# A graph attention layer on one core: row buffers by parity in the sorting stage, and squares a tile at a time at the end

## What is computed

```python
# x (6250, 96) f32; src, dst (200000,) int32, ordered by dst; W* (96, 96); 4 heads of 24
q = (x[src] @ qW).reshape(e, 4, 24)
k = (x[dst] @ kW).reshape(e, 4, 24)
v = (x[dst] @ vW).reshape(e, 4, 24)
scores = clip(einsum('ehd,ehd->eh', q, k), -10, 10)
w = exp(scores) / (segment_sum(exp(scores), src)[src] + 1e-8)
res = segment_sum(w[:, :, None] * v, src).reshape(6250, 96)
out = layernorm(x + (x + res))        # over 96, eps 1e-5, no scale
```

## Time and profile before

| | us |
|---|---|
| median of 3 runs | 1888.74 |
| lowest, highest | 1873.3, 1890.82 |
| the profiled execution | 1897.0 |
| its span in the trace | 1895.2 |

### The profile page before, as it was taken

One profiled execution on the slowest core, in us unless ns is written; L12 is line 12 of the kernel. 1 busy time (PEld: TensorE's weight loads), 2 busy tenths in 40 slices (PEclk: granted clock), 3 DMA queues, 4 the chain that ended last, 5 costly groups with the idle time before them and its releaser, 6 DMA issues.

```text
span 1895.2 us, 56765 instructions
## 1 busy us (share of the span) xinstructions
PE 1554.5 (82%) x19964; PEld 1487.2 (78%) x19965; DVE 1485.0 (78%) x2939; ACT 1238.9 (65%) x1747; POOL 979.3 (52%) x762
## 2 busy tenths in 40 slices
PE   4845777777777777777775799999999999999990
PEld 3734777777777677777765799999999999999990
DVE  6888677777776777677751699999999999999987
ACT  3342444444444444444443799999999999999981
POOL 6231555555555655555555355555555555555550
PEclk8657888898898988888887899999999999999995
DMA  5673777777777777777675976777777777777731
GB/s 174 216 269 142 269 272 270 273 277 278 276 291 271 291 284 281 268 276 276 271 272 210 333 242 226 246 242 239 237 239 241 241 242 240 238 239 241 242 126 51
DMA packets 159447, 464.98 MB, mean 245 GB/s; under 512 B 36994, under 2 KB 59266, under 8 KB 152244
## 3 DMA queue, kind: packets, MB, share of 16 engines
q1 hardware_dynamic: 123572, 301.16, 48.7%
q0 software_dynamic: 35840, 163.36, 21.4%
HBM read 271.21 MB, written 209.73 MB: 254 GB/s over the span
## 4 chain that ended last, share of the span: by engine, by line
PE 64%; DMA 14%; DVE 8%; issue 6%; ACT 4%; POOL 2%; SPq 2%; ACTq 0%; POOLq 0%; DVEq 0%
DMA sorted_rows<-work 13%; PE two_a L1088 12%; PE meta L1150 11%; PE sum_bank L1150 11%; PE two_b L1088 10%; PE two_a L1171 6%; PE two_b L1171 6%; ACT work L875 3%; PE one_d L1161 3%; PE one_c L1161 3%; POOL sorted_rows L615 2%; SPq L798 1%; DVE cols_work L1271 1%; DVE work L1197 1%; DVE work L1204 1%
## 5 line engine op out<-in xcount | busy, mean ns | idle before, releaser
L615 POOL DMA_INDIRECT sorted_rows<-work x448 | 472.6, 1055 | 426.4 <-issue 327.1
L676 POOL TENSOR_TENSOR work<-work 128x768 f32<-128x768 f32 x236 | 448.4, 1900 | 359.7 <-ACT work L912 359.7
L921 ACT ACTIVATE work<-work 128x1024 f32<-128x1024 bf16 x236 | 501.1, 2123 | 0.0
L1088 PE MATMUL two_a<-work 128*128 128x192 bf16 x2688 | 310.8, 275 | 194.3 <-ACT work L875 194.2
L1088 PEld LDWEIGHTS two_a<-work 128*128 128x128 f16 x2688 | 250.8, 109 | 222.0 <-ACT work L875 207.2
L1088 PE MATMUL two_b<-work 128*128 128x192 bf16 x2688 | 301.2, 270 | 0.0
L1088 PEld LDWEIGHTS two_b<-work 128*128 128x128 f16 x2688 | 257.0, 108 | 9.3
L875 ACT ACTIVATE work<-two_a 128x768 f32<-128x768 f32 x224 | 180.6, 806 | 106.1 <-PE two_a L1088 106.1
L1150 PE MATMUL sum_bank<-work 128*128 128x100 f32 x1888 | 235.3, 278 | 1.7 <-DVE acc L1503 1.5
L1150 PE MATMUL meta<-work 128*128 128x100 f32 x1888 | 235.3, 278 | 0.8 <-DVE acc L1503 0.8
L1534 DVE TENSOR_REDUCE work<-work 128x32 f32<-128x768 f32 x236 | 225.0, 953 | 8.2
(11 more groups left out here) (229 smaller groups left out, 2357.1 us busy)
## 6 DMA issues: line engine op xcount, KB each, us to landing
work<-sorted_rows SPq DMA_DIRECT2D x472, 392.0 KB, 3.5
work<-sorted_local SPq DMA_DIRECT2D x56, 1024.0 KB
sorted_rows<-pad_rows SPq DMA_DIRECT2D x49, 392.0 KB, 4.6
work<-kv_table SPq DMA_DIRECT2D x112, 144.0 KB, 2.2
sorted_rows<-work POOLq DMA_INDIRECT x448
kv_table<-work SPq DMA_DIRECT2D x12, 576.0 KB, 3.4
work<-in_x SPq DMA_DIRECT2D x12, 192.0 KB, 3.8
out<-acc SPq DMA_DIRECT2D x4, 576.0 KB
```

Source lines behind the costliest of these rows:

```text
L615: pool.indirect_dma_start(out=rows_dram, out_offset=bass.IndirectOffsetOnAxis(ap=place_now[:, u, b:b + 1], axis=0), in_=payload[:, u, b * ...
L676: pool.tensor_tensor(now[:, :, 0:D].rearrange("p c (h f) -> p c h f", h=HEADS), blk[:, k, :, :, D:2 * D].rearrange("p m c (h f) -> p (m c) ...
L921: act.activation(hot_f[:, k % HOTF], hot[:, k % HOTS].rearrange("p n c -> p c n"), ACT.Copy).then_inc(hotf_made[k % PSEM], 1)
L1088: mm = pe.matmul(to, picked[:, u % 2, k * P:(k + 1) * P], window[:, u, :, n, :], start=(n == 0), stop=(n == 2))
```

## The change

payload, place_now and the scattered semaphores get one copy for even and one for odd steps; sorted_v gets 8 slots in place of 4; the loops write out two steps a turn, so that the parity p is known when the kernel is built. `moved_out` waits for the scatters of step c - 2. Three semaphores go (edge_pads, flag_made, local_kept), and their signals go to dve_step or away. Scratch arrays of stage 1 move in the shared SBUF tensor to make room. At the end: chunks of 15, 14, 12 and 8 tiles in place of 12, 12, 12 and 13; POOL divides chunks 2 and 3; ACT squares tile by tile with -mean as bias and the sum in accum_out; the reciprocal is taken before the root, chunk by chunk; and the mean's subtraction and the scaling are one instruction a tile. The order of the chunks is interleaved between DVE and ACT.

```diff
-        payload, at = share(0, [QUAD, NCH, WROW], F32)
+        payload, at = share(0, [2, QUAD, NCH, WROW], F32)
...
-        sorted_v, at = share(at, [4, QUAD, TW], F32)
+        sorted_v, at = share(at, [8, QUAD, TW], F32)
...
-        place_now, at = share(at, [QUAD, RB], F32)
+        place_now, at = share(at, [2, QUAD, RB], F32)
...
-        scattered = sems("scattered", QUAD)
+        scattered = [sems(f"scattered{p}_", QUAD) for p in range(2)]
...
-            with eng.Fori(4, NQ - 1) as a:
-                emit(eng.snap(a), eng.snap(a - 1), eng.snap(a - 3))
+            with eng.Fori(2, NQ // 2 - 1) as i:
+                for p in range(2):
+                    a = eng.snap(i * 2 + p)
+                    emit(a, eng.snap(a - 1), eng.snap(a - 3), 1 - p)
+            emit(NQ - 2, NQ - 3, NQ - 5)
...
-        def moved_out(eng, u, c):
-
-            if not zero(c):
-                eng.wait_ge(scattered[u], times(eng, c, 16 * RB))
+        def moved_out(eng, u, c, p):
+
+            if not (isinstance(c, int) and c < 2):
+                eng.wait_ge(scattered[p][u], times(eng, c, 8 * RB, -8 * RB * p))
...
-                        out=rows_dram, out_offset=bass.IndirectOffsetOnAxis(ap=place_now[:, u, b:b + 1], axis=0),
-                        in_=payload[:, u, b * RUN:(b + 1) * RUN, :].rearrange("p k w -> p (k w)"), in_offset=None,
-                        bounds_check=last_place, oob_is_err=False).then_inc(scattered[u], 16)
+                        out=rows_dram, out_offset=bass.IndirectOffsetOnAxis(ap=place_now[:, p, u, b:b + 1], axis=0),
+                        in_=payload[:, p, u, b * RUN:(b + 1) * RUN, :].rearrange("p k w -> p (k w)"), in_offset=None,
+                        bounds_check=last_place, oob_is_err=False).then_inc(scattered[p][u], 16)
...
-                with pool.Fori(0, NQ) as c:
-                    fast(c)
+                with pool.Fori(0, NQ // 2) as i:
+                    for p in range(2):
+                        fast(pool.snap(i * 2 + p), p)
...
+            pool.wait_ge(stat_made, STAT_INV)
+            for c in DIVIDED:
+                divide(pool, c).then_inc(divided, 1)
...
+            def squares(c):
+
+                lo, hi = CHUNKS[c]
+                act.wait_ge(stat_made, STAT_MEAN[c])
+                for t in range(lo, hi):
+                    act.activation(sq_all[:, t, :], acc[:, t, 0:D], ACT.Square, bias=stat[:, 1, t:t + 1],
+                                   accum_out=stat[:, 2, t:t + 1]).then_inc(square_made, 1)
+
+            def root(c):
+                lo, hi = CHUNKS[c]
+                act.wait_ge(stat_made, STAT_VAR[c])
+                act.activation(stat[:, 4, lo:hi], stat[:, 3, lo:hi], ACT.Sqrt).then_inc(square_made, 1)
+
+            squares(0)
+            squares(1)
+            root(0)
+            squares(2)
+            root(1)
+            squares(3)
+            root(2)
+            root(3)
...
+            def variances(c):
+                lo, hi = CHUNKS[c]
+                dve.wait_ge(square_made, SQUARES[c])
+                link(dve.tensor_scalar(stat[:, 3, lo:hi], stat[:, 2, lo:hi], 1.0 / D, EPS_LN, ALU.mult, ALU.add))
+                dve.reciprocal(stat[:, 3, lo:hi], stat[:, 3, lo:hi]).then_inc(stat_made, 1)
+
+            def normed(c):
+                lo, hi = CHUNKS[c]
+                dve.wait_ge(square_made, ROOTS[c])
+                for t in range(lo, hi):
+                    y = acc[:, t, 0:D]
+                    ins = dve.tensor_scalar(y, y, stat[:, 1, t:t + 1], stat[:, 4, t:t + 1], ALU.add, ALU.mult)
+                    ins.then_inc(y_made, 1)
+
+            means(0)
+            means(1)
+            variances(0)
+            means(2)
+            normed(0)
+            variances(1)
+            means(3)
+            normed(1)
+            variances(2)
+            normed(2)
+            variances(3)
+            normed(3)
```

More of the change, by code:

```diff
@@ L108, in gnn_program @@
     assert FULL + NT <= NBLK and FULL <= 512 and PIECES == 7 and TI == 12 and COLS * P <= 2048
-    CHUNKS = [(NT * c // 4, NT * (c + 1) // 4) for c in range(4)]
+    CUTS = (0, 15, 29, 41, NT)
+    CHUNKS = list(zip(CUTS, CUTS[1:]))
+    DIVIDED = (2, 3)
     kv3 = nc.dram_tensor("kv3_table", (NTAB, 3 * 2 * D), BF16).ap()
@@ L256, in gnn_program @@
         flag_f, at = share(at, [1], F32)
+        parts3, at = share(at, [2, TSLOT, 3, 3, D], BF16)
+        last3, at = share(at, [3, 3, D], BF16)
+        zeros_b, at = share(at, [3 * 2 * D], BF16)
+        weights, at = share(at, [3 * D], F32)
+        select_h, at = share(at, [LO, 2, UP], F16)
+        group_h, at = share(at, [LO, HG], F16)
+        low_row, at = share(at, [LO, HG * COLS], F16)
+        diag, at = share(at, [ITERS], F32)
         assert at <= MOVE_END
@@ L600, in _ @@
             pool.wait_ge(tails_out, 16 * NT)
-            pool.memset(payload[:, :, :, TAG + 1:WROW], 0.0).then_inc(pads_made, 1)
+            pool.memset(payload[:, :, :, :, TAG + 1:WROW].rearrange("p o u c w -> p (o u c) w"), 0.0).then_inc(pads_made, 1)
             pool.wait_ge(pads_made, 2)
@@ L659, in slow @@
                         pool.sem_inc(pool_turn, 1)
-                    scatter(u, at_c)
+                    scatter(u, at_c, p)
             with pool.If(over == 0):
-                with pool.Fori(0, NQ) as c:
-                    fast(c)
+                with pool.Fori(0, NQ // 2) as i:
+                    for p in range(2):
+                        fast(pool.snap(i * 2 + p), p)
             with pool.Else():
-                with pool.Fori(0, NQ) as c:
-                    slow(c)
+                with pool.Fori(0, NQ // 2) as i:
+                    for p in range(2):
+                        slow(pool.snap(i * 2 + p), p)
             def weigh(j, drain=False):
@@ L702, in _ @@
                 sp.dma_start(weights[0:D, n * D:(n + 1) * D], w).then_inc(loads, 16)
-            sp.wait_ge(edge_pads, 2)
+            sp.wait_ge(dve_step, 2)
             for flat, held in ((src, edge_i), (dst, dest_i)):
@@ L862, in _, with emit @@
             act.activation(q3[0:NREST, FULL_NT], last3[0:NREST, 2], ACT.Copy).then_inc(q_kept, 1)
-            def emit(a, b, c):
+            def emit(a, b, c, p=None):
                 if c is not None:
+                    p = parity(c, p)
                     done_c = counts(act, c, G2, 1)
-                    at_c = bass.ds(low_bits(act, c, 3), 1)
+                    at_c = bass.ds(low_bits(act, c, 7), 1)
                 def rows(u):
-                    moved_out(act, u, c)
-                    act.activation(payload[:, u, :, TAG], sorted_v[:, at_c, u, 0:NCH].rearrange("p o w -> p (o w)"),
+                    moved_out(act, u, c, p)
+                    act.activation(payload[:, p, u, :, TAG], sorted_v[:, at_c, u, 0:NCH].rearrange("p o w -> p (o w)"),
                                    ACT.Copy).then_inc(tag_kept[u % GSEM], 1)
@@ L1401, in place @@
                     group_done(dve, dest_made, u, done_c)
-                    moved_out(dve, u, c)
+                    moved_out(dve, u, c, p)
                     with nc.allow_low_precision(reason="whole numbers below 2**24"):
-                        dve.tensor_reduce(place_now[:, u], dest_ps[:, u], AX.X, ALU.add).then_inc(place_made[u % GSEM], 1)
+                        dve.tensor_reduce(place_now[:, p, u], dest_ps[:, u], AX.X, ALU.add).then_inc(place_made[u % GSEM], 1)
                 def quad_of(t, q):
@@ L1542, in _, with means @@
             link(dve.tensor_scalar(inv, acc[:, 0:NT, D:AW], EPS_W, None, ALU.add))
-            link(dve.reciprocal(inv, inv))
+            dve.reciprocal(inv, inv).then_inc(stat_made, 1)
+            dve.wait_ge(stat_made, STAT_INV)
             dve.wait_ge(loads, 48 + 32)
-            for lo, hi in CHUNKS:
+            def means(c):
+                lo, hi = CHUNKS[c]
                 y = acc[:, lo:hi, 0:D]
-                y4 = y.rearrange("p t (h f) -> p t h f", h=HEADS)
-                link(dve.tensor_tensor(y4, y4, inv[:, lo:hi].unsqueeze(3).to_broadcast([P, hi - lo, HEADS, DH]),
-                                        ALU.mult))
+                if c in DIVIDED:
+                    dve.wait_ge(divided, DIVIDED.index(c) + 1)
+                else:
+                    link(divide(dve, c))
```

84 lines of the change are left out of this document (33 added, 51 removed).

## The result

The changed kernel takes 1708.99 us (median of 4 runs, 1703.4 to 1711.48), the kernel before 1887.72 beside it (4 runs): a ratio of 0.906, 95% interval 0.901 to 0.911. The forecast was 1688 us with a range of 1636 to 1772. The profiled execution took 1711.48 us (span 1709.3), to be set against 1897.0 (span 1895.2) before: 185.9 us of span less, where the prediction's sum was 201.

What follows compares the result with a forecast made beforehand. The prediction took a ring of one row buffer per group to bound the sorting stage, then the DMA engines. Gains 181 + 15.5 - 1.5 + 6 = 201 us off 1888.7 gave 1688 us, range 1636 to 1772.

Steps and rivals of the forecast that it cites:

- The cause: Sorting stage: one row buffer per group makes copy, issue, flight and refill follow each other, 15.48 us a step.
- The next bound: Sorting step with second buffers: DMA engines largest at 11.6 us, with POOL 11.3, DVE 10.8 to 11.3, PE 10.3.
- Rival (b): Sorting: transfers keep up and DVE is the bound, 10.8 to 11.5 us a step; 1636 us at 11.0; chance 0.23.
- Rival (d): Sorting: the wait only changes its name, pace within 0.4 us of 15.48; 1870 to 1889 us; chance 0.04.
- Rival (e): Sorting: DVE's fast f16 instructions hold up POOL's scatter issues, 16.9 us a step; 1941 us; chance 0.04.
- The pace: 52 sorting steps: 12.0 us each instead of 15.48, range 11.0 to 13.5, a gain of 181 us.
- rival (c): Sorting: transfers fall behind, packets or window loads land late, 12.6 to 14.2 us a step; 1766 at 13.5; chance 0.19.
- The three last steps: End of sorting: DVE and brow's load gone, POOL sets 10.6 us a step instead of 15.75, gaining 15.5 us.
- The last landing: End of sorting: the last scatters land behind a fuller queue, costing 1.5 us of the gain.
- The loops: Sorting loops written out two steps a turn: 0 us a step, bounds -0.2 and +0.2.
- The end: After the last addition to acc: work leaves DVE, ACT squares tile by tile; gain 6 us, bounds 0 and 9.
- POOL's division is hidden: At the end: POOL's division of chunks 2 and 3 takes 2.9 us, ready by 1857, needed at 1862.7.

Runs made afterwards that it cites:

- run 1: Changed kernel, but each write of a row or place buffer waits for the scatters of the step before, not two before; 1908.63 us, ratio 1.009.
- run 3: Changed kernel with half the bytes in each scatter, as many issues, sums left out; 1661.02 us.
- run 5: Changed kernel loading only an eighth of brow from step 2 on, sums not the right ones; 1665.09 us.
- run 4: Changed kernel with window buffers by parity, both window loads issued ahead of the store of local rows and of brow; 1728.29 us, ratio 0.915.
- run 7: Changed kernel with window buffers by parity, store of local rows first, then both windows, then brow; 1704.16 us, ratio 0.900.
- run 12: Changed kernel with parity window buffers (store, windows, brow), all end divisions on VectorE and the root's table fetched before the squares; 1698.63 us, ratio 0.897.
- run 8: Kernel before with only its sorting loops written out two steps a turn, one buffer and old end kept; 1940.60 us, ratio 1.025.
- run 2: Changed kernel with the old end (chunks, squares, norm and divisions as before); 1715.38 us, ratio 0.906.
- run 6: Changed kernel with all end divisions on VectorE and none on POOL; 1706.30 us.

## Why the prediction was right, and where its terms were off

**The cause: right.** One buffer per group made a ring; run 1 puts back only that wait and gets 15.76 us a step.

**The next bound: right in name.** The prediction took the DMA engines at 11.6 us and expected a share above 0.9; it is 0.96, and taking bytes away from either queue (runs 3, 5) lifts the bound. POOL was put at 11.3 and measures 11.36 to 11.38. TensorE's clock was expected near 1.0 and is 0.97 to 0.99. Rival (b)'s pace of 10.8 to 11.5 is reached when bytes are taken out, but POOL's issues are the bound then, not VectorE, which has 0.4 us left in a step. Rival (d) is out. Rival (e)'s mechanism exists, in part: issues beside f16 passes last 1.3 to 1.9 us, and the mean of all went from 1.055 to 1.119 us. Its price was overrated: 16 us a step by the prediction's estimate, where POOL manages 11.36 in run 5. The prediction also read the wrong pass. The issue at 655.42 lies beside L1366 and the start of L1393 as well as L1425, and the one of 1.81 us beside all three. In run 5, where the steps are even, 51 issues that lie beside L1471 alone (L1425 before) take 1.08 us, 51 beside L1439 and L1442 (L1393 and L1396, the picks) and L1478 take 1.31, and 51 beside the picks and L1411 (L1366) take 1.49. So the picks lengthen an issue more than the one-hot L1425 does.

**The pace: 12.0 predicted, 12.22 measured, 52 x 0.22 = 11.5 us less gain.** The term that was mis-sized is what the prediction added to 11.6 for the waits between engines. 0.96 x 12.22 = 11.7 us is the transfers' own work; the other 0.5 is, by this reading, what late transfers leave idle, a window behind brow 8.75 us after its issue. The upper bound of 13.5 us rested on packets that stretch; they did not (436 ns for 423). What grew is the time in the queue. The prediction looked at the wrong load: it said that a landing of 10 us was allowed to brow, and did not ask that of window 1, which is issued behind brow and needed soonest. That is rival (c)'s mechanism at a small size; runs 4 and 7 show that it can't be ordered away.

**The three last steps: 10.6 predicted, 11.94 measured, 4 us.** The step that failed is "the 1 MB load of brow is gone". SP's issues in that stretch:

```profile
812.26 0.33 SPq L800 DMA_DIRECT2D work<-sorted_local  x1
815.79 0.34 SPq L770 DMA_DIRECT2D work<-kv_table  x1
...
824.63 0.33 SPq L800 DMA_DIRECT2D work<-sorted_local  x1
```

Two more loads of brow lie in it, with windows behind them. The steps take 11.98, 13.38 and 10.46 us: only the last is as predicted. Run 5, in which these loads are an eighth as long, has 10.70 us a step there.

**The last landing: 1.5 us predicted, nothing measured.** The first load of blocks is issued 3.72 us after the last scatter's issue, 3.70 before. In runs 7 and 12 it is 4.91 and 4.49, so the term exists, but not here. That the queue had emptied with the loads gone is not shown.

**The loops: 0 taken.** In the kernel before they cost 0.5 us a step and 17 us of attention (run 8), well beyond the bounds of 0.2. In the changed kernel neither shows, and the 12.22 leave room for no more than the 0.6 us over the transfers' 11.6. In runs 3 and 5, without the wait for transfers, 8 x (1.109 + 0.30) accounts for the step without a term for the loops. That it came out at 0 was not due to an argument: the same edit in the other kernel did cost time, and the prediction had nothing that could tell the two apart.

**The end: 6 predicted, 4.1 measured** (runs 1 and 2 agree). The squares were put at 0.25 us a tile and cost 0.36, between that and the bound of 0.50: the sum does have an instruction of its own, 0.19 us long, half of it beside the square. And "POOL's division is hidden" failed: it held VectorE's first 2x + y up by 1.8 us, which run 6 takes back. By the rule of the Trainium skill, "SBUF — State Buffer" (SBUF: two separate sides), POOL's division would wait for VectorE's and then block the next pass for its own length. The rows agree: POOL's ends at 1673.81, and VectorE's pass, 1.66 us by itself, ends 1.52 us later.

## What to carry to other kernels

A ring of one buffer shows as a wait passed from engine to engine with none of them full; a second buffer takes it out at once, and the gain is found by asking what each engine and the DMA engines need per step, of which the largest is the floor. Once the DMA engines are full, reordering a queue only renames the wait (three orders, 12.06 to 12.49 us a step); fewer bytes are what helps (11.37). Giving POOL a share of VectorE's elementwise work on SBUF is no gift while VectorE does the same: time both together before counting it as hidden.

## What the runs showed of the hardware

A scatter's flight was 4.5 us in the kernel before. With the DMA engines at 0.97 it is some 13 us; in the chain of run 12, 400 to 425 us (start, length):

```profile
386.66 13.49 DMA sorted_rows<-work
...
405.98 13.20 DMA sorted_rows<-work
```

That is above the length of a step (11.99 us), and in runs 7 and 12 ACT waits for these scatters again, 148 and 149 us in all. In the changed kernel no such wait is left; its windows are late first. The packets themselves take no longer than before, so the flight grew by waiting in queues.

The rate in the full stage is 350 to 354 GB/s. The Trainium skill, "DMA: Bandwidth & Descriptors" (Specifications), gives about 358 GB/s as a core's limit to HBM. The stage stays 1 to 2% under it, but the traces show no wall there: the earlier trace rows have a stretch of 404, and the page of the changed kernel has 370 in the 43 us from 214 us on. What is full is the time of the 16 engines, at a share of 0.96.

ScalarE's square of 128x96 with a sum is two instructions, 0.36 us from one tile to the next. VectorE and POOL on SBUF at once can lengthen one another by nearly the other's whole pass (0.68 to 2.00 us beside one of 1.49), and which of them pays is decided by less than a tenth of a microsecond in their order. And the kernel before took 2025 us on one chip and 1888 to 1894 on the others. The runs of other kernels on that one chip show releases that arrive late; for the kernel before itself there is no trace from there.
